# Control tables through memory: the transposition of a small table goes from TensorE to a round trip in DRAM and VectorE

## The reference

```python
# stage one, per head h
A = -exp(log_A_real) + 1j * A_imag; dtA = A * dt
K[h, l] = 2 * Re(sum_n Cc * (exp(dtA) - 1) / A * exp(dtA * l))
y = causal_convolution(u_masked, K) + u_masked * D
x = x + y * mask
# stage two, per row t of x
logits = x @ Wr.T + bias(language);  two best experts, softmax over the two
out = x @ W.T + 2.0 * sum_e gate_e * (x @ A_e.T) @ B_e.T
x = x + out
```

## Time and profile before

| | before |
|---|---|
| median of 3 runs | 644.51 us (644.13 to 648.0) |
| the profiled execution's own time | 645.27 us |
| its span, first to last instruction | 643.5 us |
| granted TensorE clock over the span | 0.991 |
| PE busy | 619.5 us (96%) |
| PEld busy | 592.7 us (92%) |
| DVE busy | 524.1 us (81%) |
| ACT busy | 437.9 us (68%) |

### The profile page before, as it was taken

One profiled execution on the slowest core, in us unless ns is written; L12 is line 12 of the kernel. 1 busy time (PEld: TensorE's weight loads), 2 busy tenths in 40 slices (PEclk: granted clock), 3 DMA queues, 4 the chain that ended last, 5 costly groups with the idle time before them and its releaser, 6 DMA issues.

```text
span 643.5 us, 12483 instructions
## 1 busy us (share of the span) xinstructions
PE 619.5 (96%) x3439; PEld 592.7 (92%) x3439; DVE 524.1 (81%) x1560; ACT 437.9 (68%) x949; POOL 34.7 (5%) x61
## 2 busy tenths in 40 slices
PE   4798989999999999999999999999999999999997
PEld 4697989999999999999999999999999999999997
DVE  7887778888888888888888888888888888887741
ACT  5788687686676768667685867668576867764421
POOL 2241000000000000000000000000000000000000
PEclk9798999999999999999999999999999999999999
DMA  6531424443233444433334443232444432331212
GB/s 182 165 106 34 75 42 75 74 73 61 52 53 56 72 73 73 73 56 54 56 54 73 73 73 66 56 58 41 73 73 73 73 58 52 51 59 42 42 33 66
DMA packets 137856, 43.41 MB, mean 67 GB/s; under 512 B 127304, under 2 KB 132208, under 8 KB 137840
## 3 DMA queue, kind: packets, MB, share of 16 engines
q1 hardware_dynamic: 132960, 27.39, 25.6%
q10 hardware_dynamic: 4880, 15.83, 10.0%
HBM read 26.35 MB, written 16.85 MB: 67 GB/s over the span
## 4 chain that ended last, share of the span: by engine, by line
DVE 32%; PE 23%; issue 22%; ACT 16%; SPq 3%; ACTq 2%; DMA 1%; DVEq 1%
DVE state L970 11%; PE pmg L1313 11%; PE pc L1248 8%; ACT swapped L555 7%; DVE xt L1011 5%; ACT state L563 2%; DVE s_lo L999 2%; DVE zo_lo L922 2%; PE pmg L1300 1%; DVE gate L1044 1%; ACTq L606 1%; ACT t_hi L539 1%; ACT zo_hi L546 1%; ACT result L600 1%; DVE angle L787 1%
## 5 line engine op out<-in xcount | busy, mean ns | idle before, releaser
L1313 PE MATMUL pmg<-w_hi,y_hi 128*128 128x384 f32 (+1 forms) x768 | 263.2, 343 | 1.7 <-DVE y_lo L1017 1.7
L1313 PE MATMUL pmg<-w_hi,y_lo 128*128 128x384 f32 (+1 forms) x768 | 259.9, 338 | 0.0
L1313 PE MATMUL pmg<-w_lo,y_hi 128*128 128x384 f32 (+1 forms) x768 | 259.7, 338 | 0.0
L1313 PEld LDWEIGHTS pmg<-w_hi,y_hi 128*128 128x128 f32 x768 | 144.2, 188 | 2.7 <-issue 2.1
L1313 PEld LDWEIGHTS pmg<-w_hi,y_lo 128*128 128x128 f32 x768 | 144.3, 188 | 0.5
L1313 PEld LDWEIGHTS pmg<-w_lo,y_hi 128*128 128x128 f32 x768 | 144.2, 188 | 0.0
L555 ACT ACTIVATE swapped<-state 64x128 f32<-64x128 f32 x192 | 59.3, 309 | 66.3 <-DVE state L970 64.9
L970 DVE SCALAR_TENSOR_TENSOR state<-swapped,scan_tab,state 128x192 f32<-128x192 f32 (+1 forms) x240 | 73.7, 348 | 16.5 <-ACT swapped L555 12.1
L600 ACT ACTIVATE result<-pmg 128x384 f32<-128x384 f32 (+1 forms) x96 | 41.7, 449 | 39.4 <-PE pmg L1300 37.2
L1017 DVE TENSOR_TENSOR y_lo<-xt,y_hi 128x1024 fp32r<-128x1024 f32 x32 | 39.2, 1225 | 20.6 <-ACT y_hi L582 19.2
L970 DVE SCALAR_TENSOR_TENSOR state<-state,scan_tab 128x64 f32<-128x64 f32 x180 | 51.3, 327 | 3.1
(11 more groups left out here) (208 smaller groups left out, 1063.5 us busy)
## 6 DMA issues: line engine op xcount, KB each, us to landing
out<-result ACTq DMA_DIRECT2D x60, 256.0 KB, 4.3
rows<-in_x SPq DMA_DIRECT2D x224, 64.0 KB, 3.6
toe<-kpad SPq DMA_DIRECT2D x30, 128.0 KB, 4.8
rows<-in_x SPq DMA_DIRECT2D x8, 256.0 KB, 3.9
rows<-in_L_cond_W SPq DMA_DIRECT2D x3, 512.0 KB, 6.5
result<-in_L_cond_W SPq DMA_DIRECT2D x3, 512.0 KB, 6.4
w_rows<-in_L_cond_W SPq DMA_DIRECT2D x2, 512.0 KB, 4.8
result<-in_L_cond_A SPq DMA_DIRECT2D x1, 512.0 KB, 5.9
```

The source lines that it names most:

```text
L1313: ins = nc.tensor.matmul(pm[:, n, 0:o1 - o0], y[s][:, c, :], w[:, c, o0:o1], start=(c == 0 and y is y_hi and w is w_hi), stop=(c == CH - 1 ...
```

## The change

- PE no longer turns Z2 from pair 4 on. SP stores two heads of Z2 to a DRAM scratch z_store and loads it back in four DMAs as 32x32 blocks (`block_powers`, in SP's step behind `load_blocks(m+4)`, for pair m+3); VectorE transposes within the blocks into an SBUF tile ct (`turn_blocks`), and `split_ct`, `low_ct` and `kernel_column` take their input from there.
- VectorE's rotation is cut into pairs (`rotate_pair`): heads 2, 3 of the duo in step m = 0 and heads 0, 1 of the next in m = 1. GpSimd stages a small table second_tab for it.
- VectorE: turn_rows(m+2) stands in step m behind the router instead of at the end of the step before; kernel_column and the toe split take the places of two hold()s in the router, and the split of the gates that of the one before merge; the first part of the scan stands in front of split_y.
- ScalarE: split_states at the head of the next step, the Exp table load (warm) in m = 1 in front of the ratio, split_turned behind the power tables, copy_states in front of split_y, the evacuations behind the first swap_odd.
- copy_states signals the even states on their own (evens_ready), and the swap reads state instead of PSUM; control and the first addition of the scan wait for evens_ready.
- PE: control(m+2) directly behind convolve(m+1), in front of add_loras; turn_gates no longer waits for clo_ready.

```diff
@@ sync
+            def block_powers(b, m, first=False):
+                n = m - FIRST_BLOCKED
+                sp.wait_ge(z2_turned, 2 * b + (n + 2))
+                if not first:
+                    sp.wait_ge(z_blocks_in, 128 * b + 64 * n)
+                sp.dma_start(bass.AP(z_store.tensor, 0, [[SPAN, P], [P * SPAN, 2], [1, SPAN]]),
+                             Z2[:, 2 * (m % 2):2 * (m % 2) + 2, :]).then_inc(z_stored, 16)
+                if first:
+                    sp.wait_ge(b_ready, 8)
+                sp.wait_ge(z_stored, 32 * b + (16 * n + 16 + START))
+                for k in range(P // SQUARE):
+                    sp.dma_start(z_blocks[k * SQUARE:(k + 1) * SQUARE, :, :, :].rearrange("p h a j -> p (h a) j"),
+                                 bass.AP(z_store.tensor, k * SQUARE, [[SPAN, SQUARE], [SQUARE * SPAN, 2 * P // SQUARE],
+                                                                      [1, SQUARE]])).then_inc(z_blocks_in, 16)
-            def step(b, m, rows_left=True):
+            def step(b, m, rows_left=True, first=False):
                 if rows_left:
                     sp.wait_ge(xt_ready, 2 * b + m + 3)
                     load_blocks(b, m + 4)
+                block_powers(b, m + 3, first)
                 store_kernel(b, m + 3)
                 load_toe(b, m + 3)
@@ gpsimd
+            def stage_second(g):
+                vec.tensor_copy(second_tab[:, :], tab[:, CC_IM, bass.ds(g * DUO + 2, 2)]).then_inc(second_staged, 1)
             with pool.Fori(1, LOOPS) as b:
-                pool.wait_ge(z2_ready, b + 2)
+                pool.wait_ge(z2_turned, 2 * b)
                 stage_gen(b + 2)
                 pool.wait_ge(scan, SCAN * (2 * b + 2))
                 stage_scan(b + 1)
+                pool.wait_ge(z2_turned, 2 * b + 1)
+                stage_second(b + 2)
@@ scalar, turn_powers
-                act.wait_ge(ct_full, 2 * g)
+                if staged:
+                    act.wait_ge(z_stored, 32 * g + (START - 16 * FIRST_BLOCKED))
+                else:
+                    act.wait_ge(ct_full, 2 * g)
@@ scalar, copy_states
-                nc.scalar.activation(state[:, :, EVENS, :], v_psum[:, :, EVENS, :], ACT.Copy)
-                swap_state(i, slice(0, CARRIED - 1, 2), v_psum).then_inc(v_copied, 1)
+                nc.scalar.activation(state[:, :, EVENS, :], v_psum[:, :, EVENS, :], ACT.Copy).then_inc(evens_ready, 1)
+                act.wait_ge(evens_ready, i + 1)
+                swap_state(i, slice(0, CARRIED - 1, 2), state).then_inc(v_copied, 1)
@@ scalar, step: the order after
    split_toe(m+1); split_states(m+1); split_ct(m+2); split_obs(m+2)
    if m == 1: warm Exp
    ratios(m); evacuate(m-1, 2); store(m-1)
    m == 0: turns_of        m == 1: swap_powers(b+2), turn_powers(b+2)
    split_turned(m+2); split_gated(m)
    m == 0: magnitudes, waves(b+2)
    copy_states(m+2); split_y(m+1); swap_odd(m+2, 0)
    evacuate(m, 0); evacuate(m, 1); swap_odd(m+2, 1); swap_odd(m+2, 2)
@@ vector
+            def turn_blocks(b, m):
+                dve.wait_ge(z_blocks_in, 128 * b + 64 * (m - FIRST_BLOCKED + 1))
+                dve.wait_ge(clo_ready, 2 * b + m)
+                vec.transpose(ct[:, :, :].rearrange("p h (a r) -> p (h a) r", r=SQUARE),
+                              z_blocks[:, :, :, :].rearrange("p h a j -> p (h a) j")).then_inc(ct_ready, 1)
+            def low_ct(b, m):
+                i = 2 * b + m
+                dve.wait_ge(chi_ready, i + 1)
+                vec.tensor_tensor(c_lo[:, :, :], ct[:, :, :], c_hi[:, :, :].bitcast(F32), ALU.subtract
+                                  ).then_inc(clo_ready, 1)
+            def kernel_column(m):
+                vec.reduce_sum(k_col[m % 2][:, :], ct[:, :, 0:MODES], axis=mybir.AxisListType.X).then_inc(k_ready, 1)
+            def rotate_pair(g, j, scalars):
+                dve.wait_ge(z_swapped, g + 1)
+                for h in (2 * j, 2 * j + 1):
+                    ins = vec.scalar_tensor_tensor(out=Z2[:, h, :], in0=z_swap[:, h, :], scalar=scalars[h - 2 * j],
+                                                   in1=Z2[:, h, :], op0=ALU.mult, op1=ALU.add)
+                ins.then_inc(z2_turned, 1)
@@ vector, scan_states
-                dve.wait_ge(v_copied, i + 1)
+                dve.wait_ge(evens_ready, i + 1)
                 add(ODDS, state, slice(0, CARRIED - 1, 2), A_RE, into=v_psum)
                 dve.wait_ge(scan, start + 1)
+                dve.wait_ge(v_copied, i + 1)
                 add(ODDS, swapped, slice(0, CARRIED - 1, 2), A_IM)
@@ vector, step: the order after
    turn_blocks(m+2); low_ct(m+2); m == 1: split_obs(m+2), powers(b+2)
    route(m) with kernel_column(m+2) behind the logits and split_toe(m+1) behind the maximum
    turn_rows(m+2); split_states(m+1); split_rows(m+2)
    m == 0: split_obs(m+2), angles(b+2)
    merge(m+1) with split_gated(m) behind the wait for the convolution
    rotate_pair(b+1, 1) or rotate_pair(b+2, 0)
    scan_states(m+2), first part; split_y(m+1); scan_states(m+2), the rest
@@ tensor
-            def turn_gates(b, m, tables_split):
+            def turn_gates(b, m, tables_split=None):
                 pe.wait_ge(gated_ready, 2 * b + m + 1)
-                pe.wait_ge(clo_ready, tables_split)
+                if tables_split is not None:
+                    pe.wait_ge(clo_ready, tables_split)
             def step(b, m, rows_left=True):
-                if rows_left:
-                    turn_powers(b, m + 2)
                 wait_y(b, m)
                 project(b, m, 0)
                 project(b, m, 1)
-                turn_gates(b, m, 2 * b + m + 3 if rows_left else PAIRS)
+                turn_gates(b, m)
                 convolve(b, m + 1)
-                add_loras(b, m)
                 if rows_left:
                     control(b, m + 2, alone=True)
+                add_loras(b, m)
                 project(b, m, 2)
                 add_lora(BANK_ORDER[2])
```

More of the change, by code:

```diff
@@ L2 @@
 from contextlib import ExitStack
+from functools import partial
 import concourse.bass as bass
@@ L366, in _ @@
             load_blocks(0, 5)
-            step(0, 1, rows_left=False)
+            step(0, 1, rows_left=False, first=True)
             with sp.Fori(1, LOOPS) as b:
@@ L723, in step @@
                     swap_powers(b + 2)
-                store(b, m - 1)
+                    turn_powers(b + 2, True)
+                if rows_left:
+                    split_turned(b, m + 2)
                 split_gated(b, m)
@@ L1003, in hold, with merge @@
                 vec.tensor_copy(held[:, :], lang_f[:, :])
-            def merge(b, m):
+            def merge(b, m, behind_conv=hold):
                 i, s = 2 * b + m, m % 2
@@ L1008, in merge @@
                 dve.wait_ge(conv_done, i + 1)
-                hold()
+                behind_conv()
                 for h in range(2):
@@ L1018, in split_y, with route @@
                                   ).then_inc(ylo_ready, 1)
-            def route(b, m):
+            def route(b, m, behind_logits=hold, behind_top=hold):
                 i = 2 * b + m
@@ L1133, in _ @@
             merge(0, 2)
-            rotate_powers(2, False)
+            rotate_pair(2, 0, [gen_scalar(CC_IM, 2, h, False) for h in range(2)])
             scanning = scan_states(0, 3)
@@ L1149, in step @@
                     powers(b + 2)
-                route(b, m)
+                if rows_left:
+                    route(b, m, partial(kernel_column, m + 2), toe_split)
+                    turn_rows(b, m + 2)
+                else:
+                    route(b, m, behind_top=toe_split)
                 split_states(b, m + 1)
@@ L1153, in step @@
                     split_rows(b, m + 2)
-                split_gated(b, m)
-                if rows_left and m == 0:
-                    split_obs(b, m + 2)
+                    if m == 0:
+                        split_obs(b, m + 2)
                 if kernels and m == 0:
                     angles(b + 2)
-                merge(b, m + 1)
-                if kernels and m == 1:
-                    rotate_powers(b + 2, True)
+                merge(b, m + 1, partial(split_gated, b, m))
+                if ahead and m == 0:
+                    dve.wait_ge(second_staged, b)
+                    rotate_pair(b + 1, 1, [second_tab[:, h:h + 1] for h in range(2)])
+                if ahead and m == 1:
+                    rotate_pair(b + 2, 0, [gen_scalar(CC_IM, None, h, True) for h in range(2)])
+                if rows_left:
+                    dve.wait_ge(scan_staged, b + m // 2 + 1)
+                    scanning = scan_states(b, m + 2)
+                    next(scanning)
                 split_y(b, m + 1)
                 if rows_left:
-                    dve.wait_ge(scan_staged, b + m // 2 + 1)
-                    for _ in scan_states(b, m + 2):
-                        pass
-                if ahead:
-                    turn_rows(b, m + 3)
+                    for _ in scanning:
+                        pass
```

(1 more changed line is left out.)

53 lines of the change are left out of this document (32 added, 21 removed).

## The result

The changed kernel takes 661.1 us in the median of 4 runs (660.3 to 662.3), the kernel before 646.0 beside it; the ratio is 1.0235 with a 95% interval of 1.0191 to 1.0279. The forecast was 643.5. The profiled execution took 661.89 us with a span of 659.8.

The account below looks back on a forecast made before the run. TensorE's queue bounds the kernel. A double step of 2 x 18.03 + 0.29 + 0.63 = 36.98 against 37.06 gives -1.0 us, then -0.4 and +0.5 at the ends: forecast 643.5 us, range 638 to 650, 8 in 10 632 to 662.

Parts of the forecast that it names:

- The rival that sat at 660: Round trip of the tables through memory binds turn_blocks and the router: 16 us slower, 660 us at 6.9; chance 0.29.
- the sentence on ScalarE: ScalarE in m = 1: power tables done at about 9.1 us after the first projection, ahead of split_turned's rows; no cost.
- The transpositions: TensorE: two matmuls leave each step, 0.22 us per step, 28 pairs, 6.2 us gained; bounds 0.14 to 0.38.
- The gates' 0.56: TensorE in m = 1: wait for late gates and the weight load behind it, 0.56 us per double step, would go.
- VectorE's chain: VectorE from logits of m = 0 to those of m = 1: 19.55 us before, 19.13 forecast; TensorE then waits for it.
- waits of 0.29 and 0.63: TensorE: LoRA waits 0.29 us for gt_lo in m = 0; in m = 1 0.52 for s_lo and 0.11 for u_lo.
- The transposition of blocks: VectorE's turn_blocks at the head of a step: 0.38 us, between 0.33 and 0.65, hidden under s_hi.
- The ends of the loop: Last two steps with rows -0.4 us; first block table, asked for right behind the prologue, +0.5, between 0 and 3.
- The round trip: SP's store and four loads of the power tables: 6.1 us taken, 5.9 to 8.2 possible, 6.3 allowed.
- The faster rival: TensorE's new waits for VectorE don't arise: 0.92 per double step, 12 us, 631.5 us; half of it 637.5; chance 0.27.
- ScalarE late with u_hi behind the power tables: ScalarE in the step: a listed sign that the forecast is wrong; no size or chance given.

Follow-up runs that it names:

- x1: The changed kernel with ScalarE's store of the results behind turns_of (m = 0) and swap_powers (m = 1) again: 644.4 us, ratio 0.999.
- x4: The kernel before, with TensorE's two transpositions of the control tables done twice in each step of pairs 4 to 31: 647.8 us, ratio 1.0045.
- x10: x6 with TensorE turning the identity twice per step where it turned the control tables before the change: 641.3 us, ratio 0.9943 to the kernel before.
- x5: x1 with split_toe and kernel_column moved from the router to behind turn_blocks, the router's two hold()s back: 637.1 us, ratio 0.9877 to the kernel before.
- x7: The changed kernel with SP's store of the power tables made twice, one after the other: 681.4 us, ratio 1.0583 to the kernel before.
- x11: x5 with split_turned and split_gated in front of swap_powers and turn_powers in m = 1, the store ahead of them: 634.4 us, ratio 0.9836.
- x6: x5 with gt_lo in m = 0 formed directly behind u_lo instead of behind the angles: 638.7 us, ratio 0.9913 to the kernel before.
- x12: x5's kernel unchanged, run once more beside x11 on the same chip: 636.4 us, ratio 0.9865 to the kernel before.

## Why the prediction was wrong

The forecast (643.5, no change) was wrong in direction and size. The rival that sat at 660 gave the time but not the mechanism: the agreement is by chance.

- *The step that failed* is the sentence on ScalarE: "ScalarE's power tables in m = 1 are done at about 9.1, ahead of the rows that split_turned needs". They were done at 311.17 - 300.73 = 10.4. The sum of the compute instructions was right (swap_powers 1.27, turn_powers 1.28). What was left out, and so put at nothing without a reason, is the store that the change moved in front of them: two DMA issues, 1.35 us in which ScalarE starts nothing. With the store moved back (x1) the tables are done at 304.39 - 295.16 = 9.23. In the trace of before I had read the issues' lines as free, which they were there, under swap_powers. u_hi, u_lo and control follow, each late by about 1.1 us in m = 1; in m = 0 turns_of ends late by the same gap, but turn_rows comes late enough to leave only 0.2. x1 undoes this move and gives 18.64 and 18.35 where I had 18.66 and 18.32.
- *The transpositions*: 0.22 per step forecast, 0.23 to 0.25 by x4 and x10. Right.
- *The gates' 0.56 goes*: right, TensorE's view of waits has no such entry any more.
- *VectorE's chain*: forecast 19.13 from router to router, m = 0 to m = 1, and waits of 0.29 and 0.63. The terms as listed add up to 19.17, 0.04 more than the sum written. x1 measures 337.41 - 318.28 = 19.13:

```profile
318.28 0.17 DVE L1096 TENSOR_TENSOR logits<-pmg,bias 128x8 f32<-128x8 f32 x1 [0.26 <-PE pmg L1391]
...
337.41 0.16 DVE L1096 TENSOR_TENSOR logits<-pmg,bias 128x8 f32<-128x8 f32 x1
```

In x1, where ScalarE is out of the way, the steps exceed the bare 18.01 by 0.34 and 0.63. Right, and x5 shows it from the other side: taking 0.41 out of each router returns 0.34 in m = 0 and 0.19 in m = 1.
- *The transposition of blocks* took 0.44, not 0.38, and lay under s_hi as assumed.
- *The ends of the loop* were off. The last two steps with rows were put at -0.4 and took 0.13 less than before, but the step behind them, not in the sum, took 0.77 more (17.56 instead of 16.79; LoRA waits 0.53 there for gt_lo). The first step, put at +0.5 for the first block table, took 0.78 more in x1, where the clock did not fall, and its waits are those for s_lo, u_lo and gt_lo, not for the blocks.
- *The round trip* was taken at 6.1 and took about 5.6; it doesn't bind (turn_blocks has no wait in the trace). As a rival it had the chance 0.29 with a price of 16 us, close to the measured one, but x7 and the trace speak against it. The Trainium skill, "DMA: Bandwidth & Descriptors", Anatomy of one DMA, had given 2.3 for the store, as an estimate; the page measured its figure on DMAs issued from GpSimd, these are issued from SP. The trace agrees with its 2.2 to landing, but the four loads need about 3.2 from the first issue to the last landing where the estimate had 2.3: they are issued one after the other over 1.79 us.
- *The faster rival* needs the new waits gone. They were not; x11 shows that they can be made to go in good part, by a different order.
- "ScalarE late with u_hi behind the power tables" stands in the prediction's list of what would make it wrong, without a price. It should have been the rival on the slower side.

Where the expected gain went, in double steps: before 37.06; without transpositions and gate waits 36.02; plus VectorE's new waits 36.99 (x1); plus the store in front of the tables 38.27. The same table trip with the orders of x11 is at 36.31.

## What to carry to other kernels

When an order is rewritten, list for each queue everything that is passed, DMA issues and their waits too, and price them by what stands behind them: two issues that are free under a long instruction cost their full length when the engine has nothing handed to it. An engine's idle slot ahead of a wait (here 0.97 us for c_hi) is the place for small work; the same work in a chain that ends at TensorE costs its length. A swap on one queue belongs to an order on another; moved alone, each of these two cost 3%.

## What the runs showed of the hardware that I had not expected

ScalarE takes instructions ahead: a DMA issue that follows a running activation in its queue overlaps it (in the kernel before 302.24 to 302.72, under the second L497, which runs from 302.33 to 302.96; the first issue, at 301.59, even starts ahead of both, though it stands behind them in the queue), but an activation behind the issues isn't started until they are through: 1.13 us for a pair, and 1.35 from the end of the evacuation that they send to the next activation. So a queue is handed over in order, and a DMA issue can still run ahead of the activations in front of it. Two transpositions of 128 columns cost TensorE 0.23 to 0.25 us in a full queue although it is 0.14 from the start of the first of them to the start of the next matmul; most of the rest (0.08) is the slower first matmul behind them. After the gap of 2.1 to 2.2 us ahead of the loop's first step, TensorE's granted clock fell in some executions (0.65 over 4 us in the changed kernel, 0.57 in x5) and stayed at 1.00 in others (the kernel before, x1, x6, and x12, which is x5's kernel).
